# A decoder kernel of twelve stages: one group of 39 sorted tiles in the last mixture, the context as a fifth 128-row block in the attention matmuls, and last sums on three engines

## The reference, cut to what matters

```python
kv_input = jnp.concatenate([x, latents], axis=1)
kv = kv_input @ Wkv
k, v = jnp.split(kv, 2, axis=-1)
sim = jnp.einsum('bhid,bhjd->bhij', q, k) * SCALE
attn = jax.nn.softmax(sim.astype(jnp.float32), axis=-1)
out = jnp.einsum('bhij,bhjd->bhid', attn, v)
```

```python
gout = xt @ Wg.T
topv, topi = jax.lax.top_k(gout, K)          # K = 2 of E = 8
w = jax.nn.softmax(topv, axis=-1)
g = jnp.einsum('th,efh->etf', xt, W1) + b1[:, None, :]
v = jnp.einsum('th,efh->etf', xt, W2) + b2[:, None, :]
h = jax.nn.silu(g) * v                        # 512 hidden features
eo = jnp.einsum('etf,ehf->eth', h, W3) + b3[:, None, :]
out = jnp.einsum('eth,te->th', eo, comb)
```

## Time and profile before

| | us |
|---|---|
| median of 3 runs | 3911.28 (3911.06 to 3914.19) |
| the profiled execution | 3942.55 |
| its span | 3940.4 |

### The profile page before, as it was taken

The page is one execution under the profiler, slowest core; times in us unless marked ns, Lnnn a source line. Parts: engine busy times, 40 slices in busy tenths (PEclk is TensorE's granted clock), DMA queues, the critical chain, the costliest instruction groups (busy, mean ns, idle before and its releaser), DMA issues. The chain is left out here.

```text
span 3940.4 us, 54458 instructions
## 1 busy us (share of the span) xinstructions
PE 3495.3 (89%) x18930; PEld 2240.6 (57%) x18930; DVE 2191.8 (56%) x5367; ACT 1495.8 (38%) x3040; POOL 1370.0 (35%) x1904
## 2 busy tenths in 40 slices
PE   7998897899999977888798999998896989995997
PEld 5675684445555566344444555555794445554896
DVE  5374444645556468666367676765234466664454
ACT  3253112433434364233244444443352144442453
POOL 2141441423323255232254444533422144442311
PEclk9999978999999988899799999999798889996998
DMA  2004001000000000000100000001221000003212
GB/s 100 1 1 123 14 1 46 1 1 1 1 1 1 13 1 24 1 1 1 49 1 1 1 1 1 1 1 76 99 80 57 4 25 1 1 1 160 71 60 84
DMA packets 48718, 108.85 MB, mean 28 GB/s; under 512 B 6660, under 2 KB 32900, under 8 KB 46404
## 3 DMA queue, kind: packets, MB, share of 16 engines
q1 hardware_dynamic: 40964, 84.88, 6.3%
q0 software_dynamic: 7488, 20.49, 1.5%
HBM read 70.67 MB, written 34.68 MB: 27 GB/s over the span
## 5 line engine op out<-in xcount | busy, mean ns | idle before, releaser
L2653 POOL TENSOR_SCALAR probs<-probs,inv_sum 128x512 f32<-128x512 f32 x640 | 437.7, 697 | 1008.3 <-DVE inv_sum L2774 1008.1
L2616 ACT ACTIVATE probs<-psum_banks,neg_max 128x576 f32<-128x576 f32 x640 | 468.5, 737 | 742.5 <-DVE neg_max L2857 742.5
L2857 DVE TENSOR_REDUCE neg_max<-psum_banks 128x1 f32<-128x576 f32 x640 | 455.0, 752 | 213.4 <-PE psum_banks L2491 206.8
L2491 PE MATMUL psum_banks<-keys_T,queries_T 64*128 64x288 f32 x2560 | 406.0, 436 | 52.5 <-ACT probs L2616 43.2
L2783 DVE COPY probs_T<-psum_banks 128x512 f32<-128x512 f32 x640 | 409.2, 681 | 4.5 <-PE psum_banks L2411 4.5
L2491 PEld LDWEIGHTS psum_banks<-keys_T,queries_T 64*128 64x128 f32 x2560 | 224.5, 189 | 269.2 <-ACT probs L2616 147.9
L2411 PE MATMUL psum_banks<-ident,probs 128*128 128x128 f32 x2560 | 356.5, 283 | 3.2 <-POOL probs L2653 2.3
L2411 PEld LDWEIGHTS psum_banks<-ident,probs 128*128 128x128 f32 x2560 | 280.3, 143 | 128.2 <-POOL probs L2653 63.3
L2441 PE MATMUL psum_banks<-probs_T,values 128*64 128x512 f32 x1280 | 310.9, 607 | 2.2 <-issue 2.2
L4404 PE MATMUL psum_banks<-sorted_T,tile_weights 128*128 128x128 f32 x2208 | 270.1, 279 | 9.2 <-ACT tile_weights L4494 4.9
L4404 PEld LDWEIGHTS psum_banks<-sorted_T,tile_weights 128*128 128x128 f32 x2208 | 262.2, 196 | 10.7 <-issue 10.6
(11 more groups left out here) (535 smaller groups left out, 6119.2 us busy)
## 6 DMA issues: line engine op xcount, KB each, us to landing
normed<-sorted_rows SPq DMA_DIRECT2D x30, 385.5 KB
sorted_rows<-zero_rows SPq DMA_DIRECT2D x8, 1028.0 KB, 14.5
w_L_experts_down<-in_L_experts_down SPq DMA_DIRECT2D x2, 4096.0 KB, 37.1
normed<-expert_outputs SPq DMA_DIRECT2D x8, 1024.0 KB, 7.9
w_L_xattn_Wkv<-in_L_xattn_Wkv SPq DMA_DIRECT2D x2, 2048.0 KB, 8.5
w_L_experts_up<-in_L_experts_up SPq DMA_DIRECT2D x1, 4096.0 KB, 13.0
sorted_rows<-zero_rows SPq DMA_DIRECT2D x4, 899.5 KB, 14.1
x_res<-in_x SPq DMA_DIRECT2D x4, 512.0 KB, 6.9
```

Of the source, the lines that this page charges most:

```text
L2491: last = pe.matmul(k.ps[:, 2 * h + a, 0:HALF], qT[r, b % 2, j, t * P:(t + 1) * P], kT[r, j, k0:k0 + HALF], start=True, stop=True)
L2616: act.activation(prob[:, g % PB, h * w:(h + 1) * w].rearrange("p (a n) -> p a n", a=2), k.ps[:, 2 * h:2 * h + 2, 0:HALF], ACT.Exp, bias=nm ...
L2653: pool.tensor_scalar(w, w, inv[:, g % 4, h:h + 1], 1.0, ALU.mult, ALU.mult).then_inc(shared, 1)
L2857: dve.tensor_reduce(nmax[:, g % 4, h:h + 1], k.ps[:, 2 * h:2 * h + 2, 0:HALF], AX.XY, ALU.max, negate=True).then_inc(maxed, 1)
```

## The change

`MIXTURES` names the groups for each of the two mixtures: (4, 12) for stage 8, as before, and (16,) for stage 11. With one group all tokens are sorted together into 39 tiles, and all 32 scatters stand on POOL in front of the first tile; the row numbers of the second copies are set after the first 16 have landed. The last scores come before any pick. In stage 11 the bias rows and the down weights are loaded behind the first two chunks of sorted rows, with waits where they are first used, and all four batches are fetched and added after the last tile. In both mixtures the ring of output rows has six buffers. In stage 8 `rank(1)` and `put(1)` come one tile earlier and `weigh(1)` one tile later, and the weights of tiles 0 and 1 are copied before the sigmoid of the second group.

The last sums after the loop (12 token tiles in stage 8, 16 in stage 11) are divided over three engines: DVE adds the first expert's rows with their gate (L4686), ACT multiplies the second expert's rows by their gate, and POOL adds the product.

In the context attention `context_values` holds each head's 64 rows in a slab of 128 partitions of which the other 64 are zero. The context matmul reads all 128 partitions, in the same form as the four before it. Two memsets on DVE set the zeros at the start of the stage.

```diff
-        vc = k.sb("context_values", [P, PAIRS, NC], st)
+        vc = k.sb("context_values", [P, 2, PAIRS, NC], st)
...
+                        if q == 0:
+                            pe.wait_ge(zeroed, 2)
...
-                                last = pe.matmul(k.ps[r, 6, :], vc[r, j, :], pTc[r, q % 2, :], start=False, stop=True)
+                                last = pe.matmul(k.ps[r, 6, :], vc[:, h, j, :], pTc[:, q % 2, :], start=False, stop=True)
...
-                            act.copy(vc[r, 4 * a:4 * a + 4, :], k.ps[r, 7, :].rearrange(
+                            act.copy(vc[r, h, 4 * a:4 * a + 4, :], k.ps[r, 7, :].rearrange(
...
                 batch_aggr(0)
+                for h in range(2):
+                    dve.memset(vc[64 - 64 * h:128 - 64 * h, h, :, :], 0.0).then_inc(zeroed, 1)
                 dve.wait_ge(ctx_loaded, 16)
...
-GROUP_TILES = (4, 12)
+MIXTURES = ((4, 12), (16,))
+HEAD = 4
+def sorted_tiles(groups):
+
+    return [(2 * n * P + E * (P - 1)) // P for n in groups]
...
-OUTPUT_RING = 4
+OUTPUT_RING = 6
...
+    GROUP_TILES = MIXTURES[turn]
     GROUPS = len(GROUP_TILES)
+    EARLY = TT if GROUPS > 1 else 0
...
                 load_sorted(0)
                 load_sorted(1)
+                if bias is not None:
+                    load_late_weights()
...
-                sp.wait_ge(combined, TT)
-                for b in range(1, B):
-                    fetch(b, TT * (b - 1))
+                if EARLY:
+                    sp.wait_ge(combined, EARLY)
+                for b in range(EARLY // TT, B):
+                    fetch(b, TT * b - EARLY)
...
+                if GROUPS == 1:
+                    pool.wait_ge(normed, NT)
+                    pool.wait_ge(indexed, 2)
+                    for t in range(NT):
+                        scatter(t, rows[:, t, :], 0, scattered_0)
+                    pool.wait_ge(copied_again, HEAD)
+                    for t in range(HEAD):
+                        scatter(t, again[:, t, :], 1, scattered_again)
+                    pool.wait_ge(scattered_0, first_scattered)
+                    late = rows[:, HEAD:NT, D:D + 1]
+                    pool.tensor_scalar(late, late, 1.0, 1.0, ALU.add, ALU.mult).then_inc(next_ids, 1)
+                    pool.wait_ge(next_ids, 1)
+                    for t in range(HEAD, NT):
+                        scatter(t, rows[:, t, :], 1, scattered_again)
...
+                for t in range(EARLY, NT):
+                    pool.wait_ge(halfway, t + 1)
+                    pool.wait_ge(second_scaled, t - EARLY + 1)
+                    pool.tensor_tensor(k.x[:, t, :], k.x[:, t, :], got[:, t - EARLY, 1, :], ALU.add).then_inc(combined, 1)
...
-                    if n == 1:
+                    if GROUPS > 1 and n == 0:
                         rank(1)
...
+                if GROUPS > 1:
+                    copy_weights(0)
+                    copy_weights(1)
+                last = GROUPS - 1
+                if from_sigmoid:
+                    act.wait_ge(scored, PIECES)
+                    act.activation(row[:, tiles_of[last], 0:E], scores[last], ACT.Sigmoid).then_inc(rowed, 1)
+                else:
+                    act.wait_ge(picked, GROUPS)
+                    act.activation(e[:, tiles_of[last], :], e[:, tiles_of[last], :], ACT.Exp).then_inc(exped, 1)
+                if GROUPS == 1:
+                    copy_weights(0)
+                    copy_weights(1)
...
+                for t in range(EARLY, NT):
+                    act.wait_ge(fetched[t // TT], 16)
+                    act.mul(got[:, t - EARLY, 1, :], got[:, t - EARLY, 1, :], gate[:, 1, t:t + 1]).then_inc(second_scaled, 1)
...
                                              in1=k.x[:, t, :], op0=ALU.mult, op1=ALU.add).then_inc(halfway, 1)
+                    if t >= EARLY:
+                        return
...
-                    if n == 1:
+                    if GROUPS > 1 and n == 0:
                         put(1)
-                        weigh(1)
                     if n >= 1:
                         make_rows(n - 1)
+                    if GROUPS > 1 and n == 2:
+                        weigh(1)
...
-                for t in range(TT, NT):
-                    combine(t, t - TT)
+                for t in range(EARLY, NT):
+                    combine(t, t - EARLY)
```

190 lines of the change are left out of this document (99 added, 91 removed).

## The result

The changed kernel takes 3921.72 us, the median of 20 runs (3917.09 to 3928.44); the kernel before, in 20 runs beside it, 3915.72 us (3909.68 to 3919.12). The ratio is 1.0017, interval 1.0010 to 1.0024: slower by some 6 us, where I had forecast 18 us faster. The profiled execution of the changed kernel has a span of 3918.6 us, that of before had 3940.4. Read side by side, the two profiles say the opposite of the two medians. That is the first thing to explain.

The account below looks back on a forecast made before the run. No single limit: TensorE's fixed order in context attention, TensorE in running mixture loops, and a scatter chain ahead of each. Terms -11.5 - 2.0 - 4.5 + 0 + 0.9 - 5.4 + 4.7 = -17.8, median 3911.28 to 3893.6 us, range 3874 to 3908.

Parts of the forecast that it names:

- context as a fifth block: Context attention, stages 4, 7 and 10: context matmul in the 128*64 form saves tile-form changes, -11.5 us.
- weights of tiles 0 and 1 (stage 8, first tile): Stage 8: copying these weights before the sigmoid removes TensorE's 2.13 us wait at the first tile, -2.0 us.
- rank and gate weights (stage 8, loop): Stage 8: reordered small DVE operations end down(1)'s 2.69 us wait and its low clock, -4.5 us, bounds 0 and -6.5.
- last sums, stage 8: End of stage 8: 12 tiles summed on three engines at 0.95 us each plus 0.6, against 11.1 before, +0.9 us.
- stage 11, first tile: Stage 11: ranks for 16 and 32 scatters before the loop put the first tile at 3688.0 instead of 3643.26, +44.7 us.
- stage 11, loop: Stage 11: first to last tile's start 212.8 us instead of 262.9, with 12.9 us of stalls counted as gone.
- stage 11, end: Stage 11: last sums of 16 tiles instead of 12, 15.8 us against 11.1, +4.7 us.
- Rival 2: Stage 11 loop: stalls belong to the loop's start, not the scatters, and stay: +12.9, 3906.5 us; chance 0.12.
- Rival 5: Stage 11: burst of 32 scatters makes POOL wait for landings, 2.82 us each, costing 49 us: 3942 us; chance 0.07.
- Rival 4: Stage 11: late weights take 37.1 us, not 16; tile 0's down matmul stands 21 us: 3915 us; chance 0.05.
- Rivals 3 and 6: Context attention: 3, exponentials' wait takes gain back, +11.5, chance 0.06; 6, 128-row form doesn't pair heads, over 3960, chance 0.02.
- ring: Stage 8: six output buffers instead of four, taken as 0; bounds +3 and -15 us.

Follow-up runs that it names:

- e5: The changed kernel, unaltered, run again beside the kernel before: 3920.62 us, ratio to before 1.0015.
- e4: The kernel before, no edit, run again in another set with a new profile: 3914.99 us, ratio 1.0002.
- e1: The kernel before with the attention edit alone (context matmul as a fifth 128-row block): 3932.53 us, ratio to before 0.9975.
- e13: The changed kernel (one group in stage 11) with sums on DVE alone and late weights loaded at the stage's start: 3927.62 us, ratio to before 0.9967.
- e2: The changed kernel with the old form of the context matmul, so the mixture edits alone: 3947.58 us, ratio to before 1.0008.
- e3: The changed kernel with both operations of the last sums on DVE alone: 3928.94 us, ratio to before 0.9970.
- e10: e6_two_groups with the last sums on three engines again: 3894.24 us, ratio to before 0.9956.
- e7: The same kernel as e13, run in another set: 3910.76 us, ratio to before 0.9987.
- sets A and D: The two sets of runs that stood at the upper (slower) level; the kernel before had medians of 3943.2 and 3939.5 us there.
- e15: The same kernel as e6_two_groups, run again in a set at the upper level: 3911.73 us, ratio to before 0.9920.
- e6_two_groups: The changed kernel with sums on DVE alone and stage 11 in two groups again, late weights kept: 3885.92 us, ratio to before 0.9926.
- e12: e6_two_groups with stage 11's late weights loaded at the stage's start, as in the kernel before: 3920.01 us, ratio to before 0.9947.

## Why the prediction was wrong, step by step

Predicted for each step, and measured at the level of the comparison (e5 against e4, one execution each):

| step | predicted | measured |
|---|---|---|
| context as a fifth block | -11.5 | -15.2 (-10.7 by the times of e1) |
| weights of tiles 0 and 1 (stage 8, first tile) | -2.0 | -2.2 |
| rank and gate weights (stage 8, loop) | -4.5 | -4.5, then +5.6 |
| ring | 0 | 0 |
| last sums, stage 8 | +0.9 | +5.9 |
| stage 11, first tile | +44.7 | +47.0 |
| stage 11, loop | -50.1 | -41.8 |
| stage 11, end | +4.7 | +7.0 |
| sum | -17.8 | +1.8 |

The two spans differ by 1.0 us and the medians of that set by 5.6; executions of one kernel lie up to 14 us apart in this set, so of such a sum a few us are chance.

- **The base.** The step that failed first was taken in one sentence: "times in the runs are shorter by the factor 0.992". The 31 us between the profiled execution and the median were not a factor. They were stalls in two places, and these were the places that I went on to count as a gain. "I count the 12.9 us of stalls as gone with them" was right for the execution that I had: at the upper level the one-group kernels have no stall in that loop (e13: 80.00 us busy of 80, shown below). At the lower level the loop of before is 258.2 us and not 266.3, so 8.1 of the 12.9 did not exist there; and 2.8 of the 12.9 were no stall but the ranks of the second group (3652.38 to 3655.20), which the change moves in front. The new loop itself came out as predicted: 213 us from the first to the 39th tile's start, with 212.8 forecast. Rival 2 (the stalls stay) names the place but not the reason. The levels are not the whole miss: at the upper one e1 and e2 add up to -6.3, a third of the forecast.
- **The last sums.** This is the step that turned the sign. The sums themselves are at 0.864 us a tile where I took 0.95, and the reason was the one given: when they overlap, DVE's 0.48 us become 0.94 and POOL's add 0.90. What I left out was POOL's drain: the sum puts nothing behind the last add in stage 8, and the 4 us of before in stage 11. The drain ends 5.9 to 6.5 us behind POOL's last instruction in these two stages, whatever that is, and the change made POOL's last instruction the last of the stage: +6.2 in stage 8, and in stage 11, where the output transfer hid the rest, 3.4. Putting the sums back on DVE gives 8 to 9 us (e3, e10), more than the whole of the measured slowdown. Before the result the row was there to be read: the drain's record of 7.6 us, shown above.
- **Rank and gate weights.** Right in size and in place, and then given back at tile 15. My bound for this step ("the wait returns one tile later") looked at the wrong distance: the wait returned 12 tiles later and on another resource, POOL's chain of 24 scatters and 8 stores. The edit brings TensorE 6.7 us forward, but the last of these scatters only 1.7 (88.7 us behind the stage's first statistics in e5, 90.4 in e4).
- **Stage 11, first tile.** Scatters, load and first tile took 48.8 us from the first scatter, 48.6 forecast. The first scatter came 3.6 us later in the stage than forecast. Half of it are scores, complete 33.8 us behind the first statistics instead of 32.0: the granted clock stayed at 0.50, and 16 of them took 3.42 us, where in the profile of before the fastest 16 took 1.95 in a stretch with 0.67. "The same instructions for them, so the same time" was wrong by that. The other half are the ranks, all at the low clock (6.83), for which I had taken the middle of both levels. Rival 5 (the burst of scatters fills something) is refuted by a pitch of 1.28 to the end of the 32. Rival 4 (late weights) had the wait, at 2.7 us instead of 21 (3.4 and 4.4 in e3 and e2); I had allowed 1.5 for it, and e7 puts its whole cost at 3.8.
- **Context.** Right, and the largest gain of the change. The change of tile form costs what the row said, and e1 isolates it. The Trainium skill, TensorEngine Tiling (Array Packing), section Key Properties, has the rule that changing the tiling mode drains TensorE; 0.13 to 0.17 us saved a step agree with it, and its advice in When to Use Tiling, to tile rows at a contraction of 64, would have been wrong here. Rivals 3 and 6 are out.

By size, from the table: stage 11's loop, with the stalls counted for the wrong level, is off by 8.3 us, the last sums of both stages by 7.3 (9.6 of drain, less what the faster pitch gave), the wait at tile 15 by 5.6 and stage 11's first tile by 2.3. The context and the first tile of stage 8 came out 3.9 better, of which e1 supports none. That makes 19.6, the distance from -17.8 to +1.8; the 3.8 from there to the medians' +5.6 are within the spread of single executions.

What stays open: why the scatter phases have stalls in some sets of runs and not in others. The runs show that it goes with the set and neither with the kernel nor with the chip, and that it comes where POOL's scatters run beside the loop (both mixtures with two groups have it; one group has only the longer wait for the late weights). It has fixed places: in the five kernels of sets A and D with the new order and a store every third scatter, tile 6 of stage 8 takes 14.0 to 14.2 us and tile 9 12.6 to 12.9, instead of 3.7. During such a stall TensorE's matmuls of one tile come singly, with nothing in the profile that releases them, and ACT and DVE stand too, while POOL's scatters go on at 1.28 us (e15):

```profile
2792.33 1.39 PE L4444 MATMUL psum_banks<-sorted_T,tile_weights 128*128 128x128 f32 x11
2793.97 0.27 PE L4444 MATMUL psum_banks<-sorted_T,tile_weights 128*128 128x128 f32 x1 [0.25 <-issue]
2794.70 0.49 PE L4444 MATMUL psum_banks<-sorted_T,tile_weights 128*128 128x128 f32 x3 [0.46 <-issue]
2795.42 0.27 PE L4444 MATMUL psum_banks<-sorted_T,tile_weights 128*128 128x128 f32 x1 [0.23 <-issue]
2802.57 3.78 PE L4460 MATMUL psum_banks<-w_L_experts_down,hidden_T 128*128 x8 [6.88 <-DVE expert_rows L4732]
...
2799.03 0.60 ACT L4557 ACTIVATE hidden_T<-psum_banks 128x512 f32<-128x512 f32 x1 [7.71 <-issue]
2799.66 0.69 DVE L4702 TENSOR_TENSOR hidden_T<-hidden_T 128x512 f32<-128x512 f32 x1 [9.62 <-issue]
```

What the three engines stand for is not in the profile, and no run here settles it.

With one group and the weights loaded early the same kind of stretch has none of this (e13, first 80 us of stage 11's loop):

```profile
3671.00:3751.00 80.00, 80.00 (x607) 76.68 (x607) 36.18 (x64) 42.05 (x44) 12.53 (x13) 0.98 0.15 46
```

The version that beats both kernels is e6_two_groups: the attention edit, the new order, the late weights, two groups in both mixtures, and the sums on DVE, 0.9926 and 0.9920 in two sets.

## What to carry to other kernels

When the profiled execution is longer than the median, find in which rows the difference lies before any of these rows is counted as a gain. An engine that gets the last work of a stage brings its own end with it: look at the time from each engine's last instruction to the barrier, not only at the work. Bringing the consumer forward gives back the gain where it meets the producer's chain, so follow the consumer until it is steady, not only over the next wait.

## What the runs showed of the hardware

In all 18 profiles POOL's drain at the end of a stage ends 0.07 us behind POOL's last instruction in the ten stages without indirect DMAs, and 5.9 to 6.5 us behind it in the two with them. It does not matter whether adds come in between: 6.44 us behind the last store and 6.46 behind the last add in stage 8. What it goes with is the group: 6.43 to 6.46 us in every stage with 78 indirect DMAs (two groups), 5.86 to 5.88 in every one with 71 (one group), whether stores or adds come last. By these two counts that is some 0.08 us for each indirect DMA of the stage; this is an estimate from two points, and no run varied the count for its own sake.

A large transfer queued ahead delays a small one: with 5 MB of weights behind it instead of ahead, the first chunk's load was issued 10.7 us earlier in the stage (e6 against e4), and 11.3 earlier in e15 than in e12, which differ in this alone.

DVE and POOL side by side on 128 by 256 elements slow each other: alone 0.48 and 0.73 us, overlapped 0.94 and 0.90, a pair every 0.864 us.
